# Transposed h kept on chip between the logits and the shared expert, a changed tile order, and gathers in pairs

## What is computed

```
h    = einsum('bct,bcd->bdt', x, weights[subject]) + bias[subject]   # tokens x 512
s    = sigmoid(h @ gate_weight.T); biased = s + expert_bias
sel  = top 4 of 16 experts, inside the best 2 of 4 groups (by biased)
w    = 2.5 * s[sel] / sum(s[sel])
out  = x + sum_e w_e * (silu(h @ g_e.T) * (h @ u_e.T)) @ d_e.T
         + (silu(h @ g_s.T) * (h @ u_s.T)) @ d_s.T                   # shared expert
```

## Time and profile before

| what | us |
|---|---|
| median of 3 runs | 910.18 (908.15 to 911.02) |
| profiled execution | 899.97 |
| its span, first to last instruction | 898.2 |
| TensorE (PE) busy | 868.8 (97%) |
| DVE busy | 496.6 (55%) |
| ACT busy | 400.8 (45%) |
| POOL busy | 434.6 (48%) |
| mean granted TensorE clock | 0.992 |

### The profile page before, as it was taken

How to read it: one execution, slowest core, us unless ns; L and a number is a source line. 1 busy time by engine, 2 the same in 40 slices (tenths; PEclk the granted TensorE clock), 3 DMA queues, 4 the chain that set the end, 5 groups by cost and what they waited for, 6 DMA issues and landing times.

```text
span 898.2 us, 19969 instructions
## 1 busy us (share of the span) xinstructions
PE 868.8 (97%) x4248; PEld 704.0 (78%) x4249; DVE 496.6 (55%) x1071; ACT 400.8 (45%) x852; POOL 434.6 (48%) x402
## 2 busy tenths in 40 slices
PE   6999999999988999999999999999999999999994
PEld 4777887888866888888888888888888878888882
DVE  1455675876544445466444755665747557464540
ACT  3675333343343343464444643554536445453341
POOL 4330121111453766554676555765655475666432
PEclk9999999999999999999999999999999999999998
DMA  7987686965899999989999899999899999999844
GB/s 227 336 294 227 148 204 142 283 141 107 152 260 215 279 241 187 182 163 223 258 227 201 155 284 220 228 224 260 186 282 205 245 267 228 210 211 186 155 60 61
DMA packets 151735, 187.75 MB, mean 209 GB/s; under 512 B 31498, under 2 KB 104722, under 8 KB 149266
## 3 DMA queue, kind: packets, MB, share of 16 engines
q0 software_dynamic: 37296, 86.95, 48.3%
q1 hardware_dynamic: 112866, 88.80, 39.0%
q10 hardware_dynamic: 1408, 10.49, 3.5%
HBM read 90.87 MB, written 65.04 MB: 174 GB/s over the span
## 4 chain that ended last, share of the span: by engine, by line
PE 89%; DMA 5%; SPq 2%; issue 1%; POOL 1%; ACT 0%; DVE 0%; POOLq 0%; ACTq 0%; DVEq 0%
PE psGU L825 49%; PE psY L825 25%; PE psH L726 4%; PE psY L751 4%; PE psT L726 3%; PE psGU L767 3%; DMA w_ring<-tok_ring 1%; DMA tok_ring<-h_rows,idx_all 1%; SPq L412 1%; DMA raw_w<-ffn_w 1%; PE psM L851 1%; DMA out<-y_ring,idx_all 1%; POOL out L547 1%; DMA cond_sb<-cond_w 0%; SPq L415 0%
## 5 line engine op out<-in xcount | busy, mean ns | idle before, releaser
L825 PE MATMUL psGU<-split_w,xT_hi 128*128 (+1 forms) x1400 | 437.3, 394 | 3.5 <-DVE split_w L1299 1.8
L547 POOL DMA_INDIRECT out<-y_ring,idx_all x143 | 232.1, 1623 | 208.1 <-SPq L453 189.8
L825 PEld LDWEIGHTS psGU<-split_w,xT_hi 128*128 128x128 f32 x1400 | 261.6, 189 | 59.9 <-issue 4.6
L825 PE MATMUL psGU<-split_w,xT_lo 128*128 (+1 forms) x700 | 274.9, 393 | 0.0
L825 PE MATMUL psY<-split_w,hidT_hi 128*128 (+1 forms) x700 | 233.3, 414 | 1.4 <-ACT y_ring L652 1.2
L1259 DVE TENSOR_TENSOR xT_lo<-psT,xT_hi 128x512 fp32r<-128x512 f32 x175 | 120.9, 691 | 192.6 <-ACT xT_hi L637 181.7
L690 ACT ACTIVATE aT<-psGU 128x256 f32<-128x256 f32 x175 | 67.3, 384 | 277.9 <-PE psGU L825 277.8
L542 POOL DMA_INDIRECT tok_ring<-h_rows,idx_all x143 | 146.7, 1026 | 54.1 <-issue 43.2
L652 ACT ACTIVATE y_ring<-psY 128x512 f32<-128x512 f32 x175 | 103.8, 594 | 144.6 <-PE psY L825 126.1
L825 PEld LDWEIGHTS psGU<-split_w,xT_lo 128*128 128x128 f32 x700 | 132.0, 189 | 28.5
L825 PE MATMUL psY<-split_w,hidT_lo 128*128 (+1 forms) x350 | 138.3, 395 | 0.0
(11 more groups left out here) (168 smaller groups left out, 473.4 us busy)
## 6 DMA issues: line engine op xcount, KB each, us to landing
x_ring<-tok_ring SPq DMA_DIRECT2D x284, 128.0 KB
raw_w<-ffn_w SPq DMA_DIRECT2D x17, 1536.0 KB, 8.4
h_rows<-tok_ring SPq DMA_DIRECT2D x32, 256.0 KB, 3.3
tok_ring<-h_rows SPq DMA_DIRECT2D x32, 256.0 KB, 3.7
out<-y_ring POOLq DMA_DIRECT2D x32, 256.0 KB, 4.8
x_ring<-x SPq DMA_DIRECT2D x24, 256.0 KB, 3.7
tok_ring<-h_rows,idx_all POOLq DMA_INDIRECT x143, 6.3
out<-y_ring,idx_all POOLq DMA_INDIRECT x143, 5.4
```

The lines of the kernel that those rows point to most:

```text
L547: pool.indirect_dma_start(out[:, :], bass.IndirectOffsetOnAxis(idx_all[:, r:r + 1], 0), y_ring[:, r % YRING, :], None, compute_op=ALU.add) ...
L825: mm = pe.matmul(dst, a[:, slot, c], w(at + col + k * H), start=(k == 0 and a is high and at == 0), stop=(k == parts - 1 and a is low))
```

## The change

TensorE no longer transposes h in the shared stage, and SP no longer loads h back. In the logits stage ACT writes each transposed tile to a place where it is kept: tiles 24 to 31 in `x_ring`, tiles 0 to 23 in `kept_w`, which lies over `split_w` (twelve tiles in place 1, twelve in place 2). `copy_xT` and `split_x` read from there. The shared stage takes tiles 24 to 31 first and then 0 to 23 (`shared_tile`), with the outputs and the copies of x in that order. The splits of the second routed expert move to later steps, since they overwrite kept tiles, and each high piece waits until those have been read. Gathers 0 to 13 come two at a time behind seven of the outputs (`GATHERS`), and the shuffles of the shared stage stand eight tiles ahead.

```diff
-EARLY_AHEAD = 6
+EARLY_AHEAD = 8
...
-HIGHS = {17: (1, 0), 18: (1, 1), 19: (1, 2), 20: (2, 0), 21: (2, 1), 22: (2, 2)}
-LOWS = {25: ((1, 0),), 26: ((1, 1), (1, 2)), 27: ((2, 0), (2, 1)), 28: ((2, 2),)}
+KEPT_IN_X = RING
+KEPT = 2 * EW // H
+KEPT_ORDER = [k * (KEPT // 2) + 2 * j + i for j in range(PIECES) for k in range(2) for i in range(2)]
+HIGHS = {17: (1, 0), 18: (1, 1), 19: (1, 2), 24: (2, 0), 28: (2, 1), 31: (2, 2)}
+LOWS = {25: ((1, 0),), 26: ((1, 1), (1, 2)), 27: ((2, 0),), 29: ((2, 1),), 31: ((2, 2),)}
...
+GATHERS = {23: (0, 1), 24: (2, 3), 25: (4, 5), 26: (6, 7), 28: (8, 9), 29: (10, 11), 30: (12, 13)}
...
+        with nc.sbuf_tensor("kept_w", [P, SPLITS * 2 * EW], F32) as kept_w:
+            pass
         split_w = sb("split_w", [P, SPLITS * 2 * EW], F32R)
...
+        def shared_tile(n):
+
+            return (n - KEPT_IN_X) % NT
+
+        def kept_xT(tile):
+
+            if tile >= NT - KEPT_IN_X:
+                return x_ring[:, tile % RING, :]
+            at = (1 + tile // KEPT) * 2 * EW + KEPT_ORDER[tile % KEPT] * H
+            return kept_w[:, at:at + H]
...
-                if n + RING - 1 < NT:
-                    load_h(n + RING - 1)
...
-                if FIRST_GATHER <= n < FIRST_GATHER + RING:
-                    r = n - FIRST_GATHER
-                    pool.wait_ge(xposed, NT - RING + r + 1)
+                    pool.wait_ge(a_xposed, NT)
+                for r in GATHERS.get(n, ()):
                     gather(r)
 
-            for r in range(RING, AHEAD):
-                gather(r)
...
-                    if n >= 3:
-                        act.wait_ge(logits_done, n - 2)
-                    act.activation(aT[:, (n + 1) % 2, :], psT[(n + 1) % 2][:], ACT.Copy
-                                   ).then_inc(a_xT_ready, 1)
+                    act.activation(kept_xT(n - 1), psT[(n + 1) % 2][:], ACT.Copy).then_inc(a_xT_ready, 1)
...
             def copy_xT(t, n):
-                if is_shared(n):
-                    act.wait_ge(xposed, t.done(1))
-                else:
+                if n == 0:
+                    act.wait_ge(a_xT_ready, NT)
+                elif not is_shared(n):
                     act.wait_ge(turned, t.done(1 - NT))
                 if n is None or n >= 2:
                     act.wait_ge(gu_done, t.done(-1))
-                act.activation(xT_hi[:, t.slot % 2, :], psT[t.slot % 2][:], ACT.Copy).then_inc(xhi_ready, 1)
+                xT = kept_xT(shared_tile(n)) if is_shared(n) else psT[t.slot % 2][:]
+                act.activation(xT_hi[:, t.slot % 2, :], xT, ACT.Copy).then_inc(xhi_ready, 1)
...
+                    act.wait_ge(xT_ready, KEPT_IN_X + (turn - 1) * KEPT + (j + 1) * (KEPT // PIECES))
                     split_high(turn, j)
...
-            def xpose(t, n):
-                pe.wait_ge(h_loaded[t.slot], (t.rnd + 1) * 16)
-                if n >= 2:
-                    pe.wait_ge(xT_ready, t.done(-1))
-                transposes(psT[t.slot % 2], tok_ring[:, t.slot, 0:H], HK).then_inc(xposed, 1)
...
-                if n is not None and n + 1 < NT:
-                    xpose(t + 1, n + 1)
                 gate_up(t, n, kept[-1], needed)
...
-            def split_x(t):
+            def split_x(t, n):
                 v.wait_ge(xhi_ready, t.done(1))
-                v.tensor_tensor(xT_lo[:, t.slot % 2, :], psT[t.slot % 2][:], xT_hi[:, t.slot % 2, :].bitcast(F32),
+                xT = kept_xT(shared_tile(n)) if is_shared(n) else psT[t.slot % 2][:]
+                v.tensor_tensor(xT_lo[:, t.slot % 2, :], xT, xT_hi[:, t.slot % 2, :].bitcast(F32),
                                 ALU.subtract).then_inc(xT_ready, 1)
```

More of the change, by code:

```diff
@@ L75 @@
 FIRST_X_COPY = 30
-FIRST_H_LOAD = 3
 WEIGHTS_STORE = 3
 FIRST_GATHER = 23
+GATHERS = {23: (0, 1), 24: (2, 3), 25: (4, 5), 26: (6, 7), 28: (8, 9), 29: (10, 11), 30: (12, 13)}
 class Tile:
@@ L307, in build @@
         slots_ready = sem("slots_ready")
-        h_loaded = [sem(f"h_loaded{s}") for s in range(RING)]
         gathered = [sem(f"gathered{s}") for s in range(RING)]
@@ L314, in build @@
         dve_clear = sem("dve_clear")
-        xposed = sem("xposed")
         shuffled = [sem(f"shuffled{s}") for s in range(RING // DUO_TILES)]
@@ L369, in load_x @@
                 sp.dma_start(x_ring[:, t.slot, :], rows(t, x_rows)).then_inc(x_in[t.slot], 16)
[L371 to L375, removed]
-                else:
-                    sp.wait_ge(xposed, n - RING + 1)
-                sp.dma_start(tok_ring[:, t.slot, 0:H], rows(t, h_rows)).then_inc(h_loaded[t.slot], 16)
             for n in range(NT):
@@ L387, in _ @@
                 sp.dma_start(rows(t, h_rows), tok_ring[:, t.slot, 0:H]).then_inc(h_stored[t.slot], 16)
[L388 to L392, removed]
             def load_raw(turn, odd):
@@ L551, in _ @@
             for n in range(NT):
-                t = tile_at(n)
-                s = t.slot % YRING
+                s = n % YRING
                 pool.wait_ge(y_ready, n + 1)
                 pool.wait_ge(x_copied[n // X_CHUNK], 16)
-                pool.dma_start(rows(t, out), y_ring[:, s, :], accum_op=ALU.add).then_inc(scattered[s], 16)
+                pool.dma_start(rows(tile_at(shared_tile(n)), out), y_ring[:, s, :], accum_op=ALU.add
+                               ).then_inc(scattered[s], 16)
                 if n == WEIGHTS_STORE:
@@ L594, in copy_x @@
             def copy_x(k):
-                chunk = slice(k * X_CHUNK * P, (k + 1) * X_CHUNK * P)
+                first = shared_tile(k * X_CHUNK)
+                chunk = slice(first * P, (first + X_CHUNK) * P)
                 act.dma_start(out[chunk, :], x_rows[chunk, :]).then_inc(x_copied[k], 16)
@@ L765, in _ @@
                         pe.wait_ge(scored, n - 3)
+                    xT = kept_xT(n - 2)
                     for k in range(HK):
-                        mm = pe.matmul(psGU[n % 2][:, 0:E], aT[:, n % 2, k * P:(k + 1) * P],
+                        mm = pe.matmul(psGU[n % 2][:, 0:E], xT[:, k * P:(k + 1) * P],
                                        gate_sb[:, k * E:(k + 1) * E], start=(k == 0), stop=(k == HK - 1))
@@ L885, in step @@
                          kept[-3] if j >= 2 else weights(t + -2, None if n is None else n - 2)[0])
-            xpose(tile_at(0), 0)
             run_tiles(pe, *FFN, step)
@@ L1363, in step @@
                 if n is None or n < LAST:
-                    split_x(t + 1)
+                    split_x(t + 1, None if n is None else n + 1)
                 if n is None or NT - 2 <= n < LAST - 1:
@@ L1393, in _ @@
             route_weights(2)
-            split_x(tile_at(0))
+            split_x(tile_at(0), 0)
             run_tiles(v, *EARLY, step)
```

## The result

The changed kernel took 878.84 us (median of 4, 876.18 to 880.36), the kernel before in the same session 909.16 us (906.58 to 911.02): ratio 0.9665, 95% interval 0.963 to 0.970. Its profiled execution took 879.03 us with a span of 877.3, at the median of its runs. The profiled one of before (899.97) had been 9.2 us under this median of 909.16. Between the profiles the gain is 20.9 us, between the medians 30.3.

A forecast was written before the change was run, and what follows sets the result against it. TensorE was taken as the bound, 97% busy. 14.8 us from transposes plus 8.6 from the seam gave 23.4 us: 876.6 us profiled, 886.8 with 10.2 carried over. Own range 884.5 to 889; 8 in 10, 882 to 897.

The forecast's parts named there:

- the sum: Whole kernel: 14.8 + 8.6 = 23.4 us saved, profiled 876.6 us, plus 10.2 us carried over to the median: 886.8 us.
- the seam: Stretch from 249.48 to 289.91 us with the first seven routed tiles: loses 10.1 us, of which 8.6 would be saved.
- Part 1: Shared stage: transposes of h removed from TensorE, 14.1 us between products plus 0.7 at the start, 14.8 us saved.
- I leave it so: First shared step: TensorE's granted clock of 0.64 after an idle stretch, taken as unchanged.
- Part 2: Copies from SBUF: shared-stage ACT copy 0.65 us, DVE subtraction 0.69 us, both covered by the product, cost 0.
- Part 3: SP's queue: 32 h loads of 256 KB removed, no step waits for one, 0 directly.
- Part 4: Later splits of the second routed expert, up to step 31: margin 0.5 us, cost 0, up to 0.7.
- Part 5: Gathers two per step and shuffles two steps earlier: shuffle waits go, 8.6 us saved, bounds 0 and 10.1.
- what is left of the seam: First routed tiles: 1.5 us of loss remaining of 10.1, for the load of raw expert 3.
- Rival B: POOL's gathers slowed to 1.74 us by DVE's SBUF inputs, sixth gather 2.9 us late, 3 us more stall, 890; chance 0.12.
- Rival A: Around the seam DMA is the bound: stalls of 10.1 us remain, only 14.8 us saved, 895.4; chance 0.22.
- Rivals C and D: C: late outputs hold y_ring, slower, chance 0.05. D: DVE replaces transposes, DMA holds the seam, no change, 910, chance 0.04.

The follow-up runs named there:

- same_b: The kernel before, unchanged, profiled once more: one run of 910.91 us, beside a median of 902.38 us for the kernel before in that session.
- after_again: The changed kernel, unchanged, run again against the kernel before: 881.93 us beside 902.64 us, ratio 0.9729.
- after_fourth: The changed kernel, unchanged, in a later session against the kernel before: 887.01 us beside 907.89 us, ratio 0.9749.
- after_third: The changed kernel, unchanged, in more rounds against the kernel before: 884.94 us beside 903.65 us, ratio 0.979.
- singles8: The changed kernel with gathers one per step and shuffles still eight tiles ahead: 894.99 us, beside 884.94 us for the changed kernel.

## Why the prediction was wrong

**The step that failed is in the sum**: "The median of the runs shown is 910.18, 10.2 above the profiled one, which I carry over unchanged". For the changed kernel that term measured -0.2 us: its profiled execution took 879.03, its median is 878.84. The 10.2 us were not a constant of the program but the difference between one execution and others of the same kernel. What such a difference can consist of, same_b shows: 3.1 us more in the seam than the first profile, 6.2 behind it, 1.7 ahead of step 2. The change works on the first and the last of these, not on the stalls behind the seam. No profile of the kernel before was taken in the first session at a time near its median, so why its changed kernel had none of the 10 us stays open.

Without that term, 876.6 us were forecast for the profiled execution and 879.03 came: 23.4 us of gain forecast, 20.9 measured. That this is so close is in part luck, because this profile had the shortest landing of raw expert 3 of four. The means over the three profiles of the kernel before and the four of the changed one tell more:

| part of the gain, us | forecast | first profiles | means |
|---|---|---|---|
| up to step 2 (0.7 + 2 x 0.47) | 1.6 | 0.80 | 1.65 |
| steps 2 to 32 (28 x 0.47) | 13.2 | 13.07 | 13.06 |
| seam | 8.6 | 7.37 | 4.06 |
| from step 46 on | 0 | -0.34 | 0.55 |
| sum | 23.4 | 20.90 | 19.32 |

As a ratio the forecast is 886.8 / 910.18 = 0.974. The intervals of after_again (0.9648 to 0.981) and after_fourth (0.9697 to 0.9802) hold it; those of after_third (0.9755 to 0.9824) and of the first comparison (0.963 to 0.970) do not.

**Part 1** was right: 13.07 us over the 28 steps of that stretch that had transposes, 0.467 each, and the first product at 83.81 us, forecast 83.95. On the clock, "I leave it so" (0.64 in the first step) held in some executions only. TensorE was idle for 1.61 us ahead of the first product, where it was 0.97 before; the granted clock over the next 4.8 us was 0.50 in six of the thirteen profiles with that wait and 0.64 to 0.70 in the other seven. In the first profile it was 0.50, which is why only 0.8 us had arrived by step 2.

**Part 2** was right: ACT's copy from SBUF took 0.62 us (estimate 0.65), DVE's subtraction 0.69, and nothing waited for them in the table steps.

**Part 3**, 0, was right on one chip and 4 us off on another.

**Part 4** was right: the first profile shows DVE's `hidT_lo` of step 30 ending at 237.7 us, 0.6 ahead of TensorE's transposes at 238.34 (margin forecast 0.5), with no wait of TensorE there.

**Part 5** is the second term that failed, on the other side. The shuffle waits did go. But the raw load, due to land by 241.9 us, landed at 242.40 in the first profile and up to 246.23 in the others: issued at 232.3 to 233.2, it took 9.75 to 13.61 us where the sum had the 9.14 of one execution of before (same_b took 10.81 for the same load). So "what is left of the seam", set at 1.5 us, measured 2.6, 6.4, 8.5 and 7.1; the kernel before lost 7.6 to 13.1. And the pairs and early shuffles are worth at most a few of the 8.6 us: with both undone the kernel took 887.53 us beside 887.01. Where the kernel with single gathers gets its 20.4 us from, beyond the 14.8 of part 1, is in part open. The reading of the old seam was a little off as well: a mean clock of 0.96 over 40.43 us is worth about 1.6 us (my estimate), not the whole 2.8 put down to it.

**A term that nobody forecast** is at the end. From the last SiLU to the first of the last three scatters the kernel before takes 5.07, 4.96 and 5.14 us, every one of the seventeen other profiles 3.19. ACT's last copy of `hidT_hi` starts 3.8 to 4.0 us after that SiLU in the kernel before, behind a down product, and 2.0 us after it in all others. Before and after:

```profile
883.65 0.38 ACT L643 ACTIVATE hidT_hi<-psH 128x256 fp32r<-128x256 f32 x1 [3.23 <-PE psY L825]
```
```profile
862.38 0.38 ACT L638 ACTIVATE hidT_hi<-psH 128x256 fp32r<-128x256 f32 x1 [1.35 <-PE psH L722]
```

These 1.9 us are part of the gain. The change does not touch that code, and no run isolates the cause.

**Rival B**, built on a rule of the Trainium skill (page "SBUF — State Buffer", section "Who interferes with whom"): some gathers of the first pairs did take long, over the 1.5 us that I had named as a sign of being wrong.

```profile
212.05 1.12 POOL L541 DMA_INDIRECT tok_ring<-h_rows,idx_all  x1 [0.53 <-issue]
213.47 1.91 POOL L541 DMA_INDIRECT tok_ring<-h_rows,idx_all  x1 [0.30 <-issue]
...
216.69 1.31 POOL L541 DMA_INDIRECT tok_ring<-h_rows,idx_all  x1 [0.30 <-issue]
218.30 0.97 POOL L541 DMA_INDIRECT tok_ring<-h_rows,idx_all  x1 [0.30 <-issue]
...
221.98 0.98 POOL L541 DMA_INDIRECT tok_ring<-h_rows,idx_all  x1 [0.30 <-issue]
```

The sixth gather went at 221.98, 1.6 us later than forecast. But 1.45 us of that are there at the first gather already (212.05 against 210.6), because the output ahead of it went at 210.67 instead of 209.2: long gathers made 0.1 us, not B's 2.9. The long gathers (1.91, 1.31 and, for the seventh, 1.72 at 224.97) start while DVE splits weights, from 212.14, 215.87 and 224.54 on, as in the kernel before; the new subtractions, the ones that the rival counts on, overlap these gathers by 0.1 us at most. So the trace fits the rule where the splits are, and shows nothing of it for the subtractions. Whether the two inputs from SBUF are the cause, no run took apart.

**Rival A** was right in part: three of four profiles of the changed kernel lose 6.4 to 8.5 us in the seam. Its price was not, since it left 14.8 us of gain, and 18.7 to 20.9 came in the later sessions. **Rivals C and D** did not occur.

## What to carry to other kernels

When one profile lies 1% from the median, profile the unchanged kernel again before a difference is taken from it: the gap can sit in stalls that the change is about, or in others that it does not touch. Two savings that end at the same transfers must not simply be added: here two kernels with one of them each gained 14.6 and 16.6 us, those with both 18.7 to 20.9. Where transfers set the pace the order of one queue decides (a raw load behind a shuffle that waits for a gather cost 10 us). Filling a wait of 1.6 us ahead of a dense stretch with idle matmuls made the start quicker in all three profiles, by at least 0.3 us; what it is worth for the whole kernel by itself is not clear of the scatter.

## What the runs showed of the hardware

The landing time of one and the same 1.5 MB load, issued at the same point of the same kernel, was 9.75, 11.29, 12.85 and 13.61 us in four executions, with DMA shares of 1.08 to 1.10 meanwhile. In singles8, where it was issued 12 us later and the share was 0.76, it landed after 6.44 us.

TensorE's granted clock is not a fixed answer to a short gap. After the same 1.61 us without work it was 0.50 of full speed (1.2 GHz) over the whole of the next 4.8 us in six profiles and rose earlier in seven, with a mean of 0.64 to 0.70. With transposes in that gap it stayed at 1.00 (2.4 GHz) in two profiles of three; in the third it stood at 0.50 from 83.73 to 86.20 us while TensorE was busy without a break.
